# A macaron block on one core: GpSimd computes only the power of the normalisation, VectorE the rest, and two chunks of x are normalised later

## The reference

```python
x = x + 0.5 * ffn(layernorm(x))      # x: 2 x 1024 tokens x 128, float32
x = x + attention(layernorm(x))      # 16 heads of 8, causal
x = x + 0.5 * ffn(layernorm(x))

def layernorm(x): return (x - mean(x)) / sqrt(var(x) + 1e-5)
def ffn(x):                          # one shared and 7 routed experts, hidden size 352
    out = expert(x, sg, su, sd)      # (silu(x @ g.T) * (x @ u.T)) @ d.T
    w = top-2 of softmax(x @ wr.T + rb), scaled to sum 1
    for e in range(7): out = out + w[..., e] * expert(x, rg[e], ru[e], rd[e])
```

## Time and profile before

| | us |
|---|---|
| median of three runs | 547.82 |
| the three runs | 542.69, 547.82, 549.03 |
| the profiled execution | 545.02 |
| its span on the core | 543.2 |
| TensorE busy | 502.0 |
| VectorE busy | 386.7 |
| ScalarE busy | 318.9 |
| GpSimd busy | 271.3 |

### The profile page before, as it was taken

The page is one execution under the profiler, slowest core; times in us unless marked ns, Lnnn a source line. Parts: engine busy times, 40 slices in busy tenths (PEclk is TensorE's granted clock), DMA queues, the critical chain, the costliest instruction groups (busy, mean ns, idle before and its releaser), DMA issues.

```text
span 543.2 us, 12861 instructions
## 1 busy us (share of the span) xinstructions
PE 502.0 (92%) x4312; PEld 364.6 (67%) x4312; DVE 386.7 (71%) x1032; ACT 318.9 (59%) x690; POOL 271.3 (50%) x417
## 2 busy tenths in 40 slices
PE   5988899999998899999999999999898899899994
PEld 2888898998855554444444445356447899899994
DVE  4795654558479999898989899874455774454835
ACT  4662444457544577878787878687665344344632
POOL 8399898676485411222313130302348898844440
PEclk9998999999999999999999999899999999899998
DMA  8932414232753634150505050300000141422213
GB/s 272 309 90 55 120 60 124 68 113 61 220 172 103 210 81 160 26 179 7 184 2 185 2 184 1 107 1 4 2 11 30 44 91 57 129 78 90 86 40 116
DMA packets 35053, 52.63 MB, mean 97 GB/s; under 512 B 6000, under 2 KB 23920, under 8 KB 34352
## 3 DMA queue, kind: packets, MB, share of 16 engines
q1 hardware_dynamic: 27632, 39.03, 24.6%
q0 software_dynamic: 4480, 9.25, 5.1%
q10 hardware_dynamic: 2880, 3.55, 2.1%
HBM read 31.93 MB, written 28.00 MB: 110 GB/s over the span
## 4 chain that ended last, share of the span: by engine, by line
PE 50%; DVE 33%; issue 8%; POOL 3%; DMA 3%; SPq 1%; ACTq 1%; ACT 1%; DVEq 0%; POOLq 0%
DVE mxp L1884 24%; PE psum L961 10%; PE psum L944 5%; PE psum L1784 5%; PE psum L922 5%; PE psum L923 5%; PE psum L924 5%; PE psum L1743 5%; PE psum L1674 2%; DMA b_p<-in_attn_c_proj_b 2%; PE psum L1684 2%; PE psum L984 1%; POOL z_rows L1248 1%; PE psum L1825 1%; DVE act L1080 1%
## 5 line engine op out<-in xcount | busy, mean ns | idle before, releaser
L1884 DVE TENSOR_REDUCE mxp<-psum 128x1 f32<-128x512 f32 (+3 forms) x320 | 179.4, 627 | 15.8 <-PE psum L1684 11.9
L1940 ACT ACTIVATE probs<-psum 128x512 f32<-128x512 f32 x256 | 136.5, 601 | 35.0 <-PE psum L1743 34.0
L1035 ACT ACTIVATE silu<-psum 128x352 f32<-128x352 f32 x107 | 49.6, 464 | 100.2 <-PE psum L924 68.4
L1080 DVE TENSOR_TENSOR act<-silu,psum 128x352 f32<-128x352 f32 x107 | 55.5, 519 | 67.1 <-ACT silu L1035 39.7
L1271 POOL DMA_INDIRECT y_rows<-ys,to_row x76 | 74.3, 977 | 51.3 <-DVE ys L1116 25.5
L1743 PE MATMUL psum<-queries,keys 32*128 32x512 f32 (+7 forms) x384 | 98.1, 416 | 1.0 <-ACT probs L1940 1.0
L961 PE MATMUL psum<-wall_f,at 128*128 (+1 forms) x648 | 91.7, 278 | 2.8 <-DVE x L1118 1.6
L1989 POOL TENSOR_SCALAR_AFFINE_SELECT probs<-probs 128x512 f32<-128x512 f32 x48 | 29.6, 638 | 122.6 <-ACT probs L1940 122.6
L961 PEld LDWEIGHTS psum<-wall_f,at 128*128 128x128 f32 x648 | 82.0, 194 | 3.6 <-issue 2.9
L1743 PEld LDWEIGHTS psum<-queries,keys 32*128 32x128 f32 (+1 forms) x384 | 50.9, 186 | 35.1 <-ACT probs L1940 16.8
L1784 PE MATMUL psum<-probs,vg 128*32 128x512 f32 (+2 forms) x640 | 73.0, 530 | 0.0
(11 more groups left out here) (253 smaller groups left out, 853.6 us busy)
## 6 DMA issues: line engine op xcount, KB each, us to landing
z_rows<-q_stack SPq DMA_DIRECT2D x12, 682.5 KB, 5.5
keys<-k_stack SPq DMA_DIRECT2D x32, 128.0 KB, 5.2
queries<-q_stack SPq DMA_DIRECT2D x8, 512.0 KB, 4.9
zg_early<-z_rows SPq DMA_DIRECT2D x44, 65.0 KB
yc<-y_rows SPq DMA_DIRECT2D x10, 256.0 KB, 2.7
zg_late<-z_rows SPq DMA_DIRECT2D x32, 65.0 KB
yc<-y_rows ACTq DMA_DIRECT2D x6, 256.0 KB, 3.0
wall_f<-in_ffn_rd SPq DMA_DIRECT2D x1, 1344.0 KB, 16.4
```

Source lines behind the costliest of these rows:

```text
L1884: e.tensor_reduce(dst, scores, AX.X, ALU.max).then_inc(K.A["taken"], 1)
L1940: e.activation(strip_of(K, w)[:, j, :], slot(K, u, d, n)[:, 0:strip_width(w)], ACT.Exp, scale=SCALE).then_inc(K.A["ex"], 1)
```

## The change

Four things are changed. GpSimd's part of a layernorm is one instruction, the power; VectorE adds epsilon behind bn_aggr, and, where ScalarE makes z, forms the negative mean times rstd in an instruction of its own behind GpSimd's power (`norm_mr_dve`). The first 1024 tokens of x are loaded in two transfers, and the filler at the start is 4 pairs of matmuls, not 7. Chunks 2 and 3 of the first layernorm move from ahead of the first job to behind the slots of part 0, with their powers in the place of two pauses in GpSimd's row of indirect transfers. The low parts of the shared expert's weights are made by GpSimd. In both FFNs SyncE reads the row numbers of two small batches at once, and in the second FFN one indirect transfer stands between the powers of chunks 2 and 3.

```diff
-WARM = 7
+WARM = 4
...
     ins.then_inc(K.NS[k]["mv"], 1)
+    e.wait_ge(K.NS[k]["mv"], VARIANCE * c + TPC + 1)
+    e.tensor_scalar(K.var_e[:, v, :], K.mv[:, v, :, 1], LN_EPS, None, ALU.add).then_inc(K.NS[k]["mv"], 1)
...
 def norm_rstd_pool(K, k, c):
+    e.wait_ge(K.NS[k]["mv"], VARIANCE * (c + 1))
+    e.tensor_tensor(K.rstd[:, v, :], K.var_e[:, v, :], K.half_neg[:, :], ALU.pow).then_inc(K.NS[k]["rstd"], 1)
+
+def norm_mr_dve(K, k, c):
     if z_on_act(k, c):
+        e, v = K.nc.vector, norm_place(k, c)
+        e.wait_ge(K.NS[k]["rstd"], c + 1)
+        e.scalar_tensor_tensor(K.mr_neg[:, v, :], K.mv[:, v, :, 0], -1.0, K.rstd[:, v, :], ALU.mult, ALU.mult)\
+         .then_inc(K.NS[k]["mr"], 1)
...
+NORM_FOR_PAUSE = {(0, TT + 1): 2, (0, 2): 3}
...
-    if g % TT > 0:
+    if (f, g) in NORM_FOR_PAUSE:
+        norm_rstd_pool(K, f, NORM_FOR_PAUSE[f, g])
+    elif g % TT > 0:
         pause_pool(K, f == 1 and t < HALF)
...
+        if j0 == WHOLE:
+            two = n + BATCHES[b + 1][1]
...
+def weights_lo_pool(K, m):
+    e, (src, hi, lo) = K.nc.gpsimd, weights_of(K, m)
+    e.wait_ge(K.w_hi, m + 1)
+    e.tensor_tensor(lo, src, hi.bitcast(F32), ALU.subtract).then_inc(K.w_lo_shared, 1)
...
-SECOND_DVE = {18: (("n_stats", 2),), 21: (("n_stats", 3),), 28: (("n_lo", 2),), 32: (("n_lo", 3),)}
+SECOND_DVE = {18: (("n_stats", 2),), 21: (("n_mr", 2), ("n_stats", 3)), 23: (("n_mr", 3),), 28: (("n_lo", 2),), 32: (("n_lo", 3),)}
...
-BETWEEN_ACT = [{0: (("query", 0), ("hi0", 2)), 1: (("hi0", 3),), 48: (("q", 0),), 50: (("q", 1),)}, {}]
+BETWEEN_ACT = [{0: (("query", 0),), 3: (("hi0", 2),), 4: (("hi0", 3),), 48: (("q", 0),), 50: (("q", 1),)}, {}]
...
-BEHIND_ACT = [{**{2 * k + 2: (("weights", m),) for k, m in enumerate(ROUTED_WEIGHTS)},
+BEHIND_ACT = [{1: (("z0", 2),), 2: (("z0", 3),), **{2 * k + 3: (("weights", m),) for k, m in enumerate(ROUTED_WEIGHTS)},
...
-FRONT_DVE = {0: (("router", (0, 0)), ("router", (0, 1))), 1: (("places", 0),), 4: (("segments", 0),),
+FRONT_DVE = {0: (("router", (0, 0)), ("router", (0, 1))), 1: (("places", 0), ("stats0", 2), ("stats0", 3), ("mr0", 2), ("mr0", 3)), 4: (("segments", 0),),
...
-BETWEEN_PE = [{0: (("query", 0), ("tr0", 2), ("places", 0)), 1: (("tr0", 3),), 3: (("logits0", 2),), 4: (("logits0", 3),)}, {1: (("proj_tr", 2), ("proj_tr", 3)), 4: (("logits", 2), ("logits", 3)), 6: (("places", 1),)}]
+BETWEEN_PE = [{0: (("query", 0), ("places", 0)), 3: (("tr0", 2),), 4: (("tr0", 3),), 5: (("logits0", 2),), 6: (("logits0", 3),)}, {1: (("proj_tr", 2), ("proj_tr", 3)), 4: (("logits", 2), ("logits", 3)), 6: (("places", 1),)}]
-BETWEEN_DVE = [{0: (("lo0", 2),), 1: (("lo0", 3),)}, {4: (("router", (1, 0)),), 6: (("places", 1),)}]
+BETWEEN_DVE = [{3: (("lo0", 2),), 4: (("lo0", 3),)}, {4: (("router", (1, 0)),), 6: (("places", 1),)}]
...
         @block.gpsimd
-            for c in range(NCH):
-                norm_rstd_pool(K, 0, c)
+            norm_rstd_pool(K, 0, 0)
+            norm_rstd_pool(K, 0, 1)
+            for m in range(SHARED_WEIGHTS):
+                weights_lo_pool(K, m)
             sort_part_pool(K, 0, 0)
...
             norm_rstd_pool(K, 2, 2)
+            sort_part_pool(K, 1, 0, 8, 9)
             norm_rstd_pool(K, 2, 3)
             ids_pool(K, 1, 1)
-            sort_part_pool(K, 1, 0, 8)
+            sort_part_pool(K, 1, 0, 9)
```

More of the change, by code:

```diff
@@ L461, in place_memory @@
     K.ld = {n: sem(f"ld_{n}") for n in ("shared", "g", "u", "d", "small", "bias", "const", "out")}
-    K.ld_x = [sem(f"ld_x{b}") for b in range(BATCH)]
+    K.ld_x = [sem(f"ld_x{c}") for c in range(3)]
     K.passed = sem("passed")
     K.consts = sem("consts")
-    K.w_hi, K.w_lo = sem("w_hi"), sem("w_lo")
+    K.w_hi, K.w_lo, K.w_lo_shared = sem("w_hi"), sem("w_lo"), sem("w_lo_shared")
     K.sw_hi, K.sw_lo = sem("sw_hi"), sem("sw_lo")
@@ L469, in place_memory @@
     K.NS = [{n: sem(f"n{k}_{n}") for n in
-                  ("bn", "mv", "rstd", "z", "tr", "hi", "lo")} for k in range(3)]
+                  ("mv", "rstd", "mr", "z", "tr", "hi", "lo")} for k in range(3)]
     K.RS = {n: sem(f"r_{n}") for n in ROUTE_STEPS}
@@ L556, in norm_z_act @@
     e, v = K.nc.scalar, norm_place(k, c)
-    e.wait_ge(K.NS[k]["rstd"], 4 * c + 4)
+    e.wait_ge(K.NS[k]["mr"], sum(z_on_act(k, before) for before in range(c + 1)))
     if k == 0 and c == 2:
@@ L1326, in rows_load_sp @@
             e.wait_ge(K.rows_known, 2 * f + (1 if b == 0 else 2))
-        _, rows = K.nc.values_load_multi_w_load_instructions(
-            K.rows_at[0:1, j0:j0 + n], engines=(mybir.EngineType.SP,), min_val=0, max_val=SORTED - P,
-            skip_runtime_bounds_check_because="a region's start and whole tiles behind it, all within the sorted rows")
+        if j0 == WHOLE:
+            two = n + BATCHES[b + 1][1]
+            _, known = K.nc.values_load_multi_w_load_instructions(
+                K.rows_at[0:1, j0:j0 + two], engines=(mybir.EngineType.SP,), min_val=0, max_val=SORTED - P,
+                skip_runtime_bounds_check_because="a region's start and whole tiles behind it, all within the sorted rows")
+            rows, known = known[:n], known[n:]
+        elif known:
+            rows, known = known, []
+        else:
+            _, rows = K.nc.values_load_multi_w_load_instructions(
+                K.rows_at[0:1, j0:j0 + n], engines=(mybir.EngineType.SP,), min_val=0, max_val=SORTED - P,
+                skip_runtime_bounds_check_because="a region's start and whole tiles behind it, all within the sorted rows")
         if j0 in (0, WHOLE):
@@ L2264, in late_act @@
         norm_hi_act(K, 0, c)
+    elif step == "z0":
+        norm_z_act(K, 0, c)
     elif step == "weights":
@@ L2297, in late_dve @@
         norm_lo_dve(K, 0, c)
+    elif step == "stats0":
+        K.nc.vector.wait_ge(K.ld_x[2], 16)
+        norm_stats_dve(K, 0, c)
+    elif step == "mr0":
+        norm_mr_dve(K, 0, c)
     elif step == "query":
@@ L2327, in late_dve @@
         norm_stats_dve(K, 1, c)
+    elif step == "n_mr":
+        norm_mr_dve(K, 1, c)
+    elif step == "mr":
+        norm_mr_dve(K, 2, c)
     elif step == "n_lo":
```

71 lines of the change are left out of this document (28 added, 43 removed).

## The result

| | before | changed |
|---|---|---|
| median | 547.73 us | 556.42 us |
| executions | 542.69, 547.64, 547.82, 549.03 | 553.15, 556.19, 556.66, 557.16 |
| profiled execution, span | 545.02, 543.2 | 556.19, 554.4 |
| TensorE, VectorE, GpSimd busy | 502.0, 386.7, 271.3 | 504.0, 389.1, 263.8 |

The changed kernel is slower: the ratio is 1.025, with a 95% interval from 1.020 to 1.029. So it lies above the ratio of the two medians, 1.016, and puts the kernel before at about 543 us (556.42 / 1.025). The medians are 8.7 us apart, the two profiled spans 11.2 us. The engines' work has hardly changed (TensorE has 2 us more, GpSimd 7.5 less), so the time went into waiting.

The account below looks back on a forecast made before the run. VectorE was taken to bound the first FFN's shared jobs, with TensorE following. Terms 0 + 8.2 + 0.7 - 0.4 + 0.4 = 8.9 us, set on 546.4, gave 555.3 us (1.6% slower), range 549.5 to 560.5.

Parts of the forecast that it names:

- Start: Up to the router, released by the landing of bias broadcast b_p at 15.58: earlier x and shorter filler change it by 0.
- Low parts on GpSimd: Shared weights' low parts at the start: about 0.9 us each, 1.8 for two, ending before the router does, cost 0.
- The hold: Behind part 0's slots VectorE waits for GpSimd's powers of chunks 2 and 3; `act` of job 1 starts 9.6 us later.
- To job 10: First FFN's shared jobs, from the hold to `act` of job 10: cold restart and moved work leave it 9.0 us late.
- to the routed jobs: From `act` of job 10 on, 0.8 us comes back from the clock, so routed jobs begin 8.2 us later.
- Small changes elsewhere: Start of attention +0.7 us, last group of attention -0.4, second FFN +0.4.
- The base: Time of the kernel before onto which the sum was set: 546.4 us, the middle of profiled execution and median.
- (a): Rival: the clock stays low up to the routed jobs, 18.9 us in all, 565 us; chance 0.12.
- (b): Rival: the old gaps before the routed jobs are won back, delay shrinks to 5.0 us, 552.1 us; chance 0.2.
- (c): Rival: nothing is won back before the routed jobs, delay 11.9 us, 559.0 us; chance 0.1.
- (d): Rival: no hold, as powers are ready when VectorE comes to them; with b_p earlier, -2.6 us, 543.8 us; chance 0.03.
- (e): Rival: a piece of the end set to nothing, such as part 1's logits, adds 2 to 3 us; no own chance.

Follow-up runs that it names:

- r1_late: Changed kernel with chunk 2 and 3's mr_neg products and all that follows from them at later steps, powers left in place; 548.35 us, ratio 1.011 to the kernel before.
- r1_again: The changed kernel timed once more, unedited, beside the kernel before; 553.03 us, ratio 1.019 to the kernel before.
- r1_mr_first: Changed kernel with the mr_neg product of attention's chunk 0 moved ahead of the mixing of chunk 1; 551.49 us, ratio 1.014 to the kernel before.
- r4_weights_later: Changed kernel with four chunks ahead, attention's mr_neg earlier, router's own bias row, 6 filler pairs, GpSimd low parts earlier; 544.70 us, ratio 0.998 to the kernel before.

## Why the prediction was wrong in its verdict and right in its main mechanism

**Start, taken as 0.** Right within a microsecond, for another reason in the first trace: the router was released by the logits, as TensorE ran at its lower speed, at 15.45. Where it did not, b_p released it (15.73 and 16.30 in r1_late and r1_again), and in r1_mr_first b_p came last in spite of the lower speed (15.79). Low parts on GpSimd: 0.93 and 0.92 us, predicted 0.9.

**The hold, 9.6 us.** Measured 9.33, in every part: slots 21.73 (22.0), first transfer 22.89 (23.0), powers done by 31.56 (31.75). The fourth transfer took 0.97 us, with no low part of weights beside it, as the row had been read; the transfer at 47.81, beside one of 1.62 us, took 1.39. The Trainium skill (SBUF — State Buffer, "Who interferes with whom") infers that such a subtraction leaves GpSimd's descriptor generation alone, so neither transfer should differ; the trace goes against that.

**To job 10, 9.0 us, and to the routed jobs, 8.2.** Measured 10.26 and 8.89 in the first pair of traces. Against the mean of both traces of the kernel before the second is 7.8. Up to `act` of job 3 the restart cost 1.76 us (5.11 from `act` of job 1 instead of 3.35), near the 1.65 put in; but the clock stood at 0.50, the lower level of 1.2 GHz, until 37 us, beyond that `act`. More came back behind job 10, 1.4 us against 0.8. That the weights' new steps can give back as much and more is what r4_weights_later shows.

**Small changes elsewhere, 0.7 us. This is the step that failed.** It went through the start of attention (0.7 predicted, 0.43 measured), its last group (-0.4 predicted; from the last maximum to the slots of part 0 it was -1.0 in the first pair of traces and -1.7 in the second) and the second FFN (0.4 predicted for the slots of part 1 behind those of part 0; by their ends 31.16 us in both traces before and 31.10 after, so nothing). It passed over the end of the first FFN, which stands in the sum with nothing. There `norm_mr_dve` of attention's chunk 0 stands behind the mixing of chunk 1, and ScalarE's z, with a silu behind it, waits for it. The missing term was 1.35 us in the first trace by the shift of `act`; by the lengths above it was between 0.1 and 1.9 in the other traces without a low clock, and over 4 in the two where the clock falls behind it. The list of instructions showed it; I asked of each product what VectorE waits for and not who waits for VectorE. The 0.8 us at the last job was missing too. The stop that goes with it is there in eight of the twelve traces of changed and edited kernels, in neither of the kernel before, and goes with none of the edits; its cause stays open.

**The base, and luck in the sum.** The sum of 8.9 us meets the 8.7 us between the medians of the first comparison, but not the 4.6 of the second, nor the 11.2 and 9.4 us between the profiled spans of the two pairs; with a term missing, the 8.7 is in part luck. The changed kernel's median, 556.42, lies 1.1 us above the 555.3 forecast. The other part of the distance between 1.6% and 2.5% is the base: I put the kernel before at 546.4, and the ratio puts it at about 543. On my base the missing 1.35 us alone would have made it 10.3 us or 1.9%, and with the 0.8 us 2.0%. So the trace shows what the sum lacked, but the size of the verdict rests as much on the base.

**The chances.** I put the bound at 10.9 us and gave 0.2 to what lies beyond, though executions of one kernel differ by 6 us or more. The ratio came out at 1.025, and later at 1.019 with an interval across the bound. At 1.6% predicted, the two cases should have had nearly even chances. Some bounds were also added up loosely: 10 + 1.65 - 5.5 - 1.4 is 4.75 and not 5.0, and the ends of the range come to 549.2 and 560.0, not 549.5 and 560.5. Nothing here hangs on that.

**The rivals.** (a) did not happen: the granted clock was at 1.00 from 40 us on. (b) and (c) did not: the routed jobs were 8.9 us late (7.8 against the mean), not 5.0 or 11.9. (d) is excluded by the two idle times. (e), a piece that I had set to nothing, is what came, with 1.35 and 0.8 us; it had been given no chance of its own.

## What to carry to other kernels

When a step is split over two engines, each half gets a place in its engine's list, and for each place ask both questions: whom it waits for and what is queued behind it, and who waits for it and what is queued ahead. Here 7 us and 1.4 us came from products of 0.15 us. A wait that stands behind a row of transfers is as long as the row; moving the two waiting products, and what hangs on them, gave 6.9 of 8.9 us back. And look inside a losing change for the part that wins: the later steps for the weights started the routed jobs 3 us earlier once the hold was gone.

## What was not expected of the hardware

With 4 filler pairs TensorE made the first four transposes in 1.09 us in 6 of 8 traces and in 0.63 in the other two; with 6 or 7 pairs in 0.60 to 0.63 in all six. The PEclk column reads 1.00 over these microseconds in either case, so this lower speed is seen in the lengths of the matmuls alone. Why the column doesn't show it is open. The first transposes in the trace after the change, and the busy time around them:

```profile
9.80 1.09 PE L598 MATMUL psum<-ident,zrow 128*128 128x128 f32 x4 [0.99 <-ACT zrow L565]
```
```profile
9.80:10.90 1.10, 1.10 (x5) 0.97 (x6) 0.40 (x2) 0.34 (x3) 0.00 (x0) 1.00 1.05 424
```

and in r1_again, the same program:

```profile
9.81 0.63 PE L598 MATMUL psum<-ident,zrow 128*128 128x128 f32 x4 [0.99 <-ACT zrow L565]
```

In attention a step with a stretch at the lower clock is 2.3 to 2.7 us longer, and two executions of one program have them in different steps and numbers (two steps in the first trace of the changed kernel, one in the second). That is more than most terms of the prediction, and it is why stages were compared here and not ends.
